# Seven block products for two matrix products of a two-stage cross-attention kernel, with one-pass scores

## What is computed

```python
q, k, v = h_english @ w_q.T, h_lojban @ w_k.T, h_lojban @ w_v.T
probs = softmax(q @ k.T / sqrt(512));  x = x + alpha * (probs @ v) @ w_o.T
...
# second layer, per batch, x and x_2 (= ctx) seen as 256 channels x 512
g_x, theta_x, phi_x = conv1x1(g, x_2), conv1x1(theta, x), conv1x1(phi, x_2)
y = (theta_x.T @ phi_x / 512) @ g_x.T
out = gamma * (w_w @ y + w_b - mean) * rsqrt(var + eps) + beta + x
```

## Time and profile before

| | us |
|---|---|
| median of 3 runs (388.55 to 388.94) | 388.59 |
| span of the profiled execution, from its first to its last instruction | 386.3 |
| the median less that span | 2.3 |
| PE busy in the span (1776 matmuls) | 381.0 |
| DVE busy | 310.8 |
| ACT busy | 205.4 |
| POOL busy | 3.7 |

### The profile page before, as it was taken

One profiled execution on the slowest core, in us unless ns is written; L12 is line 12 of the kernel. 1 busy time (PEld: TensorE's weight loads), 2 busy tenths in 40 slices (PEclk: granted clock), 3 DMA queues, 4 the chain that ended last, 5 costly groups with the idle time before them and its releaser, 6 DMA issues.

```text
span 386.3 us, 5597 instructions
## 1 busy us (share of the span) xinstructions
PE 381.0 (99%) x1776; PEld 318.6 (82%) x1776; DVE 310.8 (80%) x595; ACT 205.4 (53%) x441; POOL 3.7 (1%) x7
## 2 busy tenths in 40 slices
PE   8999999999999999999999999999999999999995
PEld 5888878888888888888888888888888888888885
DVE  4999779987599776996689866996779875996786
ACT  3477568533664267543665257452665346552553
POOL 0001000000000000000000000000000000000000
PEclk9999999999999999999999999999999999999999
DMA  8995842486375646556383556565375564043423
GB/s 242 382 331 188 285 133 54 158 296 225 116 256 145 238 141 211 182 171 217 109 271 112 214 170 198 189 198 188 123 219 181 191 190 136 15 121 144 151 87 110
DMA packets 58059, 70.37 MB, mean 182 GB/s; under 512 B 5056, under 2 KB 47936, under 8 KB 54976
## 3 DMA queue, kind: packets, MB, share of 16 engines
q1 hardware_dynamic: 56144, 67.21, 53.2%
q10 hardware_dynamic: 1904, 3.02, 2.5%
HBM read 51.32 MB, written 18.89 MB: 182 GB/s over the span
## 4 chain that ended last, share of the span: by engine, by line
PE 97%; DMA 1%; DVE 1%; ACT 0%; issue 0%; SPq 0%
PE bank L367 23%; PE bank L368 23%; PE bank L369 23%; PE bank L421 8%; PE bank L440 7%; PE bank L407 5%; PE bank L429 4%; PE bank L462 2%; PE bank L466 1%; DMA xb<-w_k 1%; DVE xb L1143 0%; DVE xb L1138 0%; PE bank L393 0%; ACT theta_hi L621 0%; ACT t_sides L621 0%
## 5 line engine op out<-in xcount | busy, mean ns | idle before, releaser
L367 PE MATMUL bank<-ov_hi,c_sides 128*128 128x512 f32 x128 | 50.0, 391 | 0.0
L368 PE MATMUL bank<-c_sides,qk_hi 128*128 128x512 f32 x128 | 49.9, 390 | 0.0
L369 PE MATMUL bank<-c_sides,qk_lo 128*128 128x512 f32 x128 | 49.9, 390 | 0.0
L368 PE MATMUL bank<-ov_lo,c_sides 128*128 128x512 f32 x128 | 49.9, 390 | 0.0
L367 PE MATMUL bank<-c_sides,qk_hi 128*128 128x512 f32 x128 | 49.8, 389 | 0.0
L369 PE MATMUL bank<-ov_hi,c_sides 128*128 128x512 f32 x128 | 49.8, 389 | 0.0
L621 ACT ACTIVATE t_sides<-bank 128x512 fp32r<-128x512 f32 x32 | 19.0, 594 | 37.2 <-PE bank L369 37.2
L421 PE MATMUL bank<-t_sides,xT_hi 128*128 128x512 f32 x128 | 31.9, 391 | 0.0
L877 DVE TENSOR_TENSOR vo_lo<-bank,vo_hi 128x512 fp32r<-128x512 f32 x32 | 21.8, 685 | 11.8 <-ACT vo_hi L621 10.9
L621 ACT ACTIVATE probs<-bank 128x512 f32<-128x512 f32 x16 | 9.4, 585 | 37.9 <-PE bank L429 37.9
L367 PEld LDWEIGHTS bank<-ov_hi,c_sides 128*128 128x128 f32 x128 | 24.1, 188 | 5.2 <-DVE wg_sides L877 0.4
(11 more groups left out here) (148 smaller groups left out, 820.9 us busy)
## 6 DMA issues: line engine op xcount, KB each, us to landing
cT_raw<-ctx_t SPq DMA_DIRECT2D x8, 1024.0 KB, 4.8
xT_raw<-x_t SPq DMA_DIRECT2D x8, 1024.0 KB, 5.1
c_raw<-ctx_n SPq DMA_DIRECT2D x8, 1024.0 KB, 6.5
xb<-x SPq DMA_DIRECT2D x16, 512.0 KB, 4.2
out<-xb SPq DMA_DIRECT2D x14, 512.0 KB, 2.8
gram_moved<-gram_blocks SPq DMA_DIRECT2D x16, 256.0 KB, 2.3
gram_blocks<-gram_moved SPq DMA_DIRECT2D x64, 64.0 KB, 2.0
moved<-blocks SPq DMA_DIRECT2D x16, 256.0 KB, 2.3
```

The lines of the kernel that those rows point to most:

```text
L367: pe.matmul(dst, ahi, bhi, start=(k == 0), stop=False)
L368: pe.matmul(dst, ahi, blo, start=False, stop=False)
L369: mm = pe.matmul(dst, alo, bhi, start=False, stop=(k == k_tiles - 1))
```

## The change

Two of the products of each pair, t and the values, are 512x512 by 512x512 when both batches are taken together. Both are cut in 2x2 blocks of 256 and computed with seven block products in place of eight (the scheme of Winograd's form of Strassen's algorithm). Seven products M1 to M7, each 12 matmuls of 256 columns (`half_product`), go into PSUM banks called chain, join and seed. This needs:

- four sums of blocks of the folded weights (S1, N2, S3, S4), made once in the setup with their high and low parts;
- four sums of context blocks (T1, N2C, T3, N4C) for each pair, made on POOL (`mix_sum`) in `mix_raw`, which is the buffer of the natural context, then a high part each on ACT (`mix_part`) and a low part each: T1 and N2C on DVE, T3 and N4C on POOL;
- sums between the products in PSUM: ACT copies the chain bank into the seed bank (`copy_chain`) and the join bank into SBUF (`keep_join`), DVE adds twice (`join`, `join_side`), for t and again for the values.

The scores go into one bank of 512 columns per batch, with three matmuls of 256 columns per step (`scores`). ACT's copy and DVE's addition of the two halves fall away: maximum and exponential read the bank. `w_g_phi` is cut the same way, and `t1_rows` loses an addition. On ACT `c_sums` moves to the start of the pair, since the context sums overwrite its buffer; the load of that buffer waits for the last low part of the sums. x1 now shares the buffer of the values, and theta that of pT. In the setup ACT makes the high parts of w_o, which DVE made before; the loads of small parameters come later, the bias of the second layer is a small matmul in place of POOL's two calculations, and the combined weights (`combine_w_g`) are computed within the first pair, whose order is written out by itself.

```diff
+FIRST_SUMS = 4
+PRODUCTS = 7
+M1, M2, M3, M4, M5, M6, M7 = range(PRODUCTS)
+A11, A12, S4, A22, S1, N2, S3 = range(PRODUCTS)
+T1, N2C, T3, N4C = range(4)
+MIXED_SIDE = {M4: N4C, M5: T1, M6: N2C, M7: T3}
...
-        x1 = split("x1", [P, 2, KL, H])
+        x1 = vo
+        mix = split("mix", [P, 4, KS, S])
...
-        theta = split("theta", [P, 2, H])
+        theta = [t[:].rearrange("p b x n -> p b (x n)") for t in pT]
...
+        mix_raw = c_raw[:].rearrange("p b k (c s) -> p (b k) c s", c=KS)
...
-            def t_tile(m):
-                product(bank[TT_BANK[m]][:].rearrange("p (b s) -> p b s", b=2), lambda k: cut(qk, every, k, tile(m)),
-                        lambda k: cut(cT, every, k),
-                        KH).then_inc(tT_done, 1)
-            def high_scores(b, at_k, stop=False):
+            def context(i, kt):
+                if i in MIXED_SIDE:
+                    return cut(mix, every, MIXED_SIDE[i], kt)
+                k, b = {M1: (kt, 0), M2: (2 + kt, 0), M3: (2 + kt, 1)}[i]
+                return cut(cT, every, k, b)
+            def half_product(dst, lhsT, rhs, opens):
+                for n in range(2):
+                    for kt in range(2):
+                        (ahi, alo), (bhi, blo) = lhsT(n, kt), rhs(n, kt)
+                        at = dst[:, n * S:(n + 1) * S]
+                        pe.matmul(at, ahi, bhi, start=(opens and n == 0 and kt == 0), stop=False, skip_group_check=True)
+                        pe.matmul(at, ahi, blo, start=False, stop=False, skip_group_check=True)
+                        mm = pe.matmul(at, alo, bhi, start=False, stop=(kt == 1), skip_group_check=True)
+                return mm
+            def t_product(i, to_bank, opens=False):
+                half_product(bank[to_bank], lambda n, kt: cut(qk, every, i, kt, tile(n)),
+                             lambda n, kt: context(i, kt), opens).then_inc(tT_done, 1)
+            def v_product(i, to_bank, opens=False):
+                half_product(bank[to_bank], lambda n, kt: [t[:, tile(n)] for t in context(i, kt)],
+                             lambda n, kt: cut(ov, every, i, kt), opens).then_inc(vo_done, 1)
+            def scores(b):
                 for lt in range(KL):
-                    for k in at_k:
-                        mm = pe.matmul(banks[:, SCORE_BANK[b]][:, lt], xT[0][:, b, k, tile(lt)],
-                                       t_sides[:, k, b].rearrange("p h s -> p (h s)"),
-                                       start=(k == 0), stop=(stop and k == KH - 1))
-                return mm
-            def low_scores(b, stop=False):
-                for lt in range(KL):
+                    at = bank[SCORE_BANK[b]][:, lt * S:(lt + 1) * S]
                     for k in range(KH):
-                        mm = pe.matmul(banks[:, SCORE_BANK[b]][:, lt, 0:S], xT[1][:, b, k, tile(lt)], tT[0][:, k, b],
-                                       start=False, stop=(stop and k == KH - 1))
-                return mm
-            def values(b, st):
-                product(bank[VO_BANK[b][st]][:], lambda k: cut(cT, every, k, b, tile(st)),
-                        lambda k: cut(ov, every, k, every), KH).then_inc(vo_done, 1)
...
-                pe.wait_ge(tT_lo, four[3])
+                two, four = counts(pe, p, 2, [0, 1, 2, 3, 4]), counts(pe, p, 4, range(-2, 9))
+                pe.wait_ge(tT_lo, four[4])
+                pe.wait_ge(xT_lo, two[1])
+                scores(0)
                 pe.wait_ge(xT_lo, two[2])
+                scores(1)
                 if not first:
                     pe.wait_ge(out_made, four[-2])
-                high_scores(0, range(KH - 1))
-                pe.wait_ge(tT_lo, four[4])
-                high_scores(0, [KH - 1])
-                if not first:
-                    pe.wait_ge(out_made, four[0])
-                high_scores(1, [0])
-                low_scores(0, stop=True).then_inc(scores_done, 1)
-                low_scores(1)
-                high_scores(1, range(1, KH), stop=True).then_inc(scores_done, 1)
+                v_product(M1, VO_CHAIN, opens=True)
+                if first:
+                    pe.wait_ge(gram_read, 1)
+                    pe.wait_ge(ov_sum_lo, 2)
+                else:
+                    pe.wait_ge(phi_turned, p + 1)
+                v_product(M5, VO_JOIN, opens=True)
+                pe.wait_ge(vo_copied, two[1])
+                if first:
+                    pe.wait_ge(ov_sum_lo, 4)
+                v_product(M6, VO_CHAIN)
+                if first:
+                    pe.wait_ge(gram_read, 2)
+                v_product(M2, VO_SEED)
+                pe.wait_ge(vo_joined, two[1])
+                v_product(M7, VO_CHAIN)
+                v_product(M3, VO_JOIN)
+                pe.wait_ge(vo_joined, two[2])
+                v_product(M4, VO_CHAIN)
                 if first:
                     pe.wait_ge(small_lo, 2)
                     pe.wait_ge(gram_lo, 2)
                     phi_gram(FIRST_PHI_BANK)
-                    pe.wait_ge(wg_lo, 1)
                 else:
-                    pe.wait_ge(phi_turned, p + 1)
-                for st in range(KS):
-                    values(0, st)
-                if first:
-                    pe.wait_ge(phi_turned, p + 1)
-                else:
-                    pe.wait_ge(scores_summed, two[2])
+                    pe.wait_ge(out_made, four[0])
                     pe.wait_ge(u_lo, p + 1)
-                    if last:
-                        w_g_phi([0], LAST_T1_BANK[0])
-                    else:
-                        w_g_phi([0, 1], T1_BANK)
-                for st in range(KS):
-                    values(1, st)
+                    w_g_phi([0] if last else [0, 1])
...
+                if not first:
+                    pe.wait_ge(x1_made, four[2])
+                    t_product(M1, TT_CHAIN, opens=True)
+                    pe.wait_ge(mix_lo, four[5])
+                    t_product(M5, TT_JOIN, opens=True)
+                    pe.wait_ge(x1_made, four[4])
+                    theta_rows(0, [four[1], four[2]])
+                pe.wait_ge(tT_copied, two[3])
+                pe.wait_ge(mix_lo, four[6])
+                t_product(M6, TT_CHAIN)
+                t_product(M2, TT_SEED)
...
+                pe.wait_ge(tT_joined, two[3])
+                pe.wait_ge(mix_lo, four[7])
+                t_product(M7, TT_CHAIN)
                 pe.wait_ge(gram_read, two[4])
-                t_tile(2)
                 pe.wait_ge(t1_lo, two[1])
                 pe.wait_ge(theta_lo, two[1])
                 for ct in range(KL):
                     output(0, ct)
-                t_tile(3)
-                pe.wait_ge(tT_lo, four[5])
+                t_product(M3, TT_JOIN)
+                pe.wait_ge(tT_joined, two[4])
+                pe.wait_ge(mix_lo, four[8])
+                t_product(M4, TT_CHAIN)
...
+            def copy_chain(to_bank, from_bank, done, count, copied):
+                act.wait_ge(done, count)
+                act.activation(bank[to_bank][:], bank[from_bank][:], ACT.Identity).then_inc(copied, 1)
+            def keep_join(side, from_bank, done, count, copied):
+                act.wait_ge(done, count)
+                act.activation(side, bank[from_bank][:].rearrange("p (n s) -> p n s", n=2), ACT.Identity).then_inc(copied, 1)
...
+                if not last:
+                    c_sums(loads[16], kept=p)
+                v_sums()
                 exp(0)
-                low_scores(1)
-                if not first:
-                    u_part()
+                if not last:
+                    xT_part(0, loads[32])
                 exp(1)
-                vo_part(0, 0)
-                if first:
-                    xT_part(0, loads[32])
-                vo_part(0, 1)
-                if first:
+                copy_chain(VO_SEED, VO_CHAIN, vo_done, seven[1], vo_copied)
+                if not last:
                     xT_part(1, loads[32])
+                keep_join(vo_side, VO_JOIN, vo_done, seven[2], vo_copied)
+                u_part()
+                if not last:
+                    cT_part(0, loads[32], seven[1])
                 pT_part(0)
+                vo_part(0, HALF[0], VO_SEED, seven[4])
+                vo_side_part()
+                vo_part(1, HALF[0], VO_JOIN, seven[6])
+                vo_part(0, HALF[1], VO_CHAIN, seven[7])
+                pT_part(1)
...
+            def join(side, join_bank, chain_bank, done, count, kept, copied, joined):
+                dve.wait_ge(copied, kept)
+                dve.wait_ge(done, count)
+                dve.tensor_tensor(bank[join_bank][:], bank[chain_bank][:], side.rearrange("p n s -> p (n s)"),
+                                  ALU.add).then_inc(joined, 1)
+            def join_side(side, chain_bank, done, count, joined):
+                dve.wait_ge(done, count)
+                dve.tensor_tensor(side, in_halves(chain_bank), side, ALU.add).then_inc(joined, 1)
...
+                weigh_sums(loads[16])
```

(49 more changed lines are left out.)

966 lines of the change are left out of this document (583 added, 383 removed).

## The result

The changed kernel takes **399.47 us** (median of 4 runs, 398.4 to 400.07) against 388.57 (4 runs, 388.42 to 388.94): 1.0276 times the time before, 95% interval 1.0259 to 1.0293. The prediction of 382.5 with a range of 378 to 391 was wrong, and on the wrong side: the kernel became slower, not faster. Times of versions are medians; one execution of `e5_weigh_later` (400.93 us at a mean granted clock of 0.989) was in the slow state and is left out of its median.

What follows compares the result with a forecast made beforehand. PE was taken as the bound, busy 381.0 of 386.3 us. Savings of 4.4 us in six loop pairs, 1.2 in setup and first pair and 0.5 in the last make 6.1: 388.6 - 6.1 = 382.5 us, range 378 to 391.

Steps and rivals of the forecast that it cites:

- PE's steps: Matmuls on PE: a 256-column step takes 0.120 us against 0.227 for 512, so half the columns cost 53%.
- The scores' part: Scores on PE: 48 matmuls of 256 columns replace 16 of 512 and 16 of 256, +0.2 us a pair, +1.7 overall.
- The untaxed step: Rival, chance 0.04: in PE's long streams 256 columns cost half a 512 step, 0.1135 us, giving 376 us.
- the -12.9 of t and values: PE's t and value products: 48 steps of 0.227 become 84 of 0.120, -0.8 us for each of sixteen.
- DVE's and ACT's sums: Work per loop pair: DVE gains net 1.6 us, to 37.3 of 42.9; ACT gains 3, to 26.4.
- POOL's price: POOL's six calculations of 512 elements: 1.6 us each, bounds 0.6 and 3.2, so 9.6 us a pair fit.
- the rival: Chance 0.20: POOL's sums hold DVE's two negatives, 0.8 us each; PE stands 1.4 us at M6, total 390 us.
- 0.6 us of waits a pair: PE in the loop: 0.2 to 0.35 us of waiting found, 0.6 taken, making a pair 43.5 us.
- four places have less slack than my times have error: PE's loop waits: the reason for taking 0.6 us a pair instead of the 0.2 to 0.35 found.
- The rival of VectorE as second bound: Chance 0.18: DVE's list slips 0.5 us, waits reach 1.1 a pair, pair 44.0, total 386.4 us.
- outside the loop: Forecast: setup and first pair keep 1.2 of 1.8 us saved, after 0.6 of waits; last pair 0.5 of 0.6.
- `c_raw`'s load: Load waits for the last low part, takes 6.5 us, lands about 1 us before the pair; ACT covered by about 1 us.

Runs made afterwards that it cites:

- e5_weigh_later: Changed kernel with DVE's `weigh_sums` moved behind the second maxima and ACT's `v_sums` behind `keep_join`; 395.46 us, 1.0147.
- e13: Changed kernel, own order, POOL's context sums, their low parts and the summed value weights' low parts cut to 8 columns per row throughout; 392.26 us, 1.0105.
- e14: e13 plus three reorderings: `weigh_sums` after second maxima, `join_side` before second `gram_close`, second gram squares before x1's low parts; 389.97 us, 1.0044.
- e18: e14 with SP's two 1 MB loads waiting for the second batch's gram blocks; 389.83 us, 1.0022.
- e17: Changed kernel, everything computed, with the three reorderings, late 1 MB loads, and POOL calculations in four pieces outside the setup; 391.81 us, 1.007.
- e12: Kernel before with only the one-pass scores: three products of 256 columns per pair of tiles, no copy or addition; 390.17 us, 1.0038.
- e15: Changed kernel with the three reorderings, POOL pieces outside the setup, and both `w_g_phi` batches ahead of delta in the last pair; 393.23 us, 1.0115.
- e9: Changed kernel with each POOL calculation of the mixed contexts written as four of 128 elements, everything computed; 395.62 us, 1.0162.
- e8: Kernel before with eight idle POOL sums of 512 elements in each loop pair, and `dynamic_dma_scratch_size=512`; 405.59 us, 1.0429.
- e1: Changed kernel with POOL's four context sums in the loop cut to 16 of 512 elements; 396.68 us, 1.0181.
- e4: Changed kernel with ACT's `copy_chain` of the values ahead of the second batch's exponentials; 398.85 us, 1.0242.
- e3: Changed kernel with POOL's four loop sums waiting until both negatives of the maxima are made; 405.6 us, 1.0436.
- e2: Changed kernel with DVE's `join_side` of t ahead of the second `gram_close`; 398.64 us, 1.0255.
- e7: Changed kernel with POOL's loop sums cut to 16 of 512 elements and `join_side` ahead of the second `gram_close`; 392.44 us, 1.0086.

## Why the prediction was wrong

Spans, with the predicted ones made from its own steps (86.4 = 87.58 - 1.2, 43.5, and 32.8 = 33.3 - 0.5):

| | to the loop | a loop pair | last pair | span |
|---|---|---|---|---|
| before | 87.6 | 44.24 | 33.3 | 386.3 |
| predicted | 86.4 | 43.5 | 32.8 | 380.2 |
| after | 91.9 | 45.30 | 34.8 | 398.5 |
| e13, POOL short | 88.0 | 44.61 | 34.9 | 390.5 |
| e14, and reordered | 88.7 | 44.17 | 34.6 | 388.3 |
| e18, and late loads | 88.5 | 44.16 | 34.5 | 388.0 |
| e17, all computed | 90.7 | 44.26 | 34.5 | 390.8 |

- **PE's steps: right.** 256 columns step at 0.120 us, also in long streams (the 24 matmuls of M6 and M2 of t, 260.43 to 263.30). The scores' part was tested alone (e12). The untaxed step is out. (Unrounded, the -12.9 of t and values is -13.1; it changes nothing.)
- **DVE's and ACT's sums: right without POOL.** 37.3 and 26.4 us a pair were predicted; DVE has 37.0 in e13 and 37.3 in e18, ACT 26.4. Joins take 0.69 a row, the forms that write PSUM cost no more than those that read it, and ACT's copy 0.59.
- **POOL's price: right kind, oversized.** 1.3 to 1.4 us each, 1.6 taken. The placement, 1.5 to 8 us of the pair, was 1.4 to 6.8.
- **What failed first: POOL was counted as free.** The forecast put at nothing what DVE loses beside POOL, and the rival charged it too narrowly: 0.8 us at each negative. The prediction's reason against that rival, that the sums are over before the first negative at 3.8 us, held for POOL calculations of 0.6 us and not for 1.3: they end at 6.8. In the loop, the changed kernel against e13, the negatives cost 0.4 a pair; the two products of `weigh_sums`, which the prediction did not place, 1.6; two low parts of t1 beside POOL's low parts 1.0. That is 3.0 us of rows, which overlap a little, and 2.7 of DVE's busy time (39.7 against 37.0). Its price over the whole kernel is 7 us (e13), of which 2.6 to 3.9 lie ahead of the loop, where POOL's low parts of the summed weights and its first sums run over DVE's last low parts of t, x_t and the gram sums. The forecast gave the setup 0.6 us of waits.
- **What failed second: 0.6 us of waits a pair.** The changed kernel has 2.4 (45.3 - 42.9). With contention gone and the order mended PE still waits 1.3 a pair (44.16 - 42.9). The waits move: `copy_chain`, `join_side`, `gram_lo` and the last low part of t were each removed once, and each time another place took part of it, in the end delta. The step "four places have less slack than my times have error" was true, but the places are in series in one list, on DVE, and each stop costs 0.1 more than itself, since the product after it takes 0.39 us and not 0.28. The rival of VectorE as second bound (44.0 a pair) describes this state; its 386.4 us expected 0.8 us saved outside the loop.
- **What failed third: outside the loop.** Even without contention the loop begins 1.6 to 2.3 us later than the predicted 86.4 (e13, e14, e18). The setup isn't at fault: the first scores begin at 41.2 to 41.4 us there, 41.7 before. The first pair is: 46.8 to 47.3 us in place of 45.9. And the last pair is 1.7 to 2.0 longer than the predicted 32.8. There PE waits 0.95 us for `vo_lo` ahead of delta; e15 filled that wait with products from the tail and gained nothing, which points at DVE or ACT. Which step ends it was not tested.
- **`c_raw`'s load: nearly right.** It held ACT by 0.6 to 0.7 us in two of the six loop pairs, and `c_sums` ended 0.2 to 1.3 us into the pair. ACT lost nothing by it, as it then waits for DVE (3.2 us in the pair shown), but this end is what starts POOL's sums just over `weigh_sums`.

Together: 17.0 us between 399.5 and 382.5; contention 7.2, the three reorderings 2.3, late loads 0.1, and 7.3 left in e18. The reorderings were priced without contention, and e14's executions spread from 388.87 to 393.41, so the split is rough. In spans the rest is 388.0 - 380.2 = 7.8: the loop has 6 x 0.66 = 4.0 of it, setup and first pair 2.1, the last pair 1.7. For the loop DVE's list is the likely cause; for the first and the last pair the cause stays open. No version that computes everything came under the kernel before; the best, e17, is 0.7% above it. Why the gram blocks land late when the big loads are held back stays open.

## What to carry to other kernels

Before you give POOL elementwise work beside a busy DVE, list DVE's instructions with two SBUF inputs in that stretch and charge each with up to nearly one whole POOL instruction (here up to 1.1 us beside POOL's 1.3); their number counts, not their size. Shorten POOL's instructions (e9), or put them beside DVE's reads of PSUM, which kept their times in e8; no run here arranges the work so. And where a change cuts the engine that bounds, take off its profit what the next list in series makes it wait: here PE's 1.35 us a pair met 1.3 us of waits that no reordering removed. Where a change adds waits, look at the granted clock of every stretch before you put a price on them.

## What the runs showed of the hardware

- Eight idle POOL sums of 1.38 us a pair, which nobody waited for, made the kernel before 17 us slower (e8): about 12 by the two engines, about 4.5 by three falls of the granted clock to 1.2 GHz, 3.41 us each, behind PE waits of 2.1 us. In e1 and e4 one such fall stands behind waits of 2.0 and 2.3 us. While it lasts, 512 columns step by 0.43 us and 256 by 0.21, in place of 0.227 and 0.120.
- DVE and POOL hold each other. Beside POOL, four DVE calculations on 128 elements took 4.37 us in place of 1.14 (e8). Beside DVE, a POOL sum of 1.29 us took up to 1.69 (e8), a low part of 1.3 us 2.31 (changed kernel, setup), a piece of 0.46 us 1.45 (e9).
- A DVE calculation on 128x2 elements from one SBUF tile (`neg_max`) waits too, 0.17 us alone and up to 0.86 in the changed kernel and 1.16 in e3, while a reduction over 512 elements from one SBUF tile doesn't (0.69 in all 16 of e8).
- Executions of one version with new waits scatter by 0.8 to 4.5 us (e2 and e14), where 17 of the kernel before lie within 1.4. In the profiled executions the pairs of one run differ by up to 2.4 us (43.41 to 45.84 in e7), the longest with waits for the gram blocks.
